# Half of the attention values computed inside the phase loop, and copied out by VectorE

## What is computed

```
q = (Q @ w_q.T).reshape(B, S, G, HG, HD)       # 8 groups of 4 heads, HD = 8
k = (K @ w_k.T).reshape(B, S, G, HD)
v = (V @ w_v.T).reshape(B, S, G, HD)
scores = jnp.einsum('bnghd,bmgd->bnghm', q, k) / scale
scores = jnp.where(causal, scores, NEG_INF)
attn = jax.nn.softmax(scores, axis=-1)
out = jnp.einsum('bnghm,bmgd->bnghd', attn, v).reshape(B, S, D)
return out @ w_o.T + b_o
```

## Time and profile before

| | |
|---|---|
| median of three runs | 400.14 us |
| the profiled execution's own time | 402.57 us |
| its span | 399.6 us |
| PE busy | 343.4 us (86%) |
| DVE busy | 210.5 us (53%) |
| ACT busy | 164.7 us (41%) |
| POOL busy | 100.9 us (25%) |

### The profile page before, as it was taken

How to read it: one execution, slowest core, us unless ns; L and a number is a source line. 1 busy time by engine, 2 the same in 40 slices (tenths; PEclk the granted TensorE clock), 3 DMA queues, 4 the chain that set the end, 5 groups by cost and what they waited for, 6 DMA issues and landing times.

```text
span 399.6 us, 4567 instructions
## 1 busy us (share of the span) xinstructions
PE 343.4 (86%) x1470; PEld 207.2 (52%) x1477; DVE 210.5 (53%) x501; ACT 164.7 (41%) x344; POOL 100.9 (25%) x156
## 2 busy tenths in 40 slices
PE   2999886529999847999799989988879989999997
PEld 1485675316665534555463655453343535444886
DVE  5143874502222267799436935792141339778921
ACT  2433443213333122246872875396785223333000
POOL 7102663520000377102340434045243001000000
PEclk9999997558999656999999999999999999999999
DMA  6995000152111127100000000000000000000011
GB/s 213 383 419 138 1 15 2 65 175 75 54 40 54 46 77 282 57 6 0 8 1 2 0 7 2 1 0 8 0 1 2 0 2 0 0 0 3 25 41 39
DMA packets 13880, 22.41 MB, mean 56 GB/s; under 512 B 2033, under 2 KB 11249, under 8 KB 13042
## 3 DMA queue, kind: packets, MB, share of 16 engines
q1 hardware_dynamic: 13090, 20.03, 14.5%
q0 software_dynamic: 768, 2.10, 1.6%
HBM read 15.83 MB, written 6.03 MB: 55 GB/s over the span
## 4 chain that ended last, share of the span: by engine, by line
PE 60%; DVE 16%; ACT 9%; issue 6%; POOL 4%; DMA 3%; another core or an unknown queue 0%; SPq 0%; ACTq 0%; DVEq 0%; POOLq 0%
PE bank L230 45%; DVE mx L1169 8%; ACT region L895 5%; PE bank L442 5%; PE bank L410 3%; POOL x_sorted L709 2%; PE bank L413 2%; DVE stats L966 2%; PE bank L243 1%; DVE x_sb L1006 1%; POOL rstd L682 1%; PE bank L237 1%; ACT qst L846 1%; DMA x_sb<-in_x_dram 1%; PE bank L490 1%
## 5 line engine op out<-in xcount | busy, mean ns | idle before, releaser
L1169 DVE TENSOR_REDUCE mx<-bank 128x2 f32<-128x512 f32 (+1 forms) x96 | 60.2, 684 | 13.9 <-PE bank L413 8.3
L895 ACT ACTIVATE region<-bank,padcol 128x512 f32<-128x512 f32 x96 | 60.7, 701 | 12.0 <-PE bank L230 11.0
L745 POOL TENSOR_SCALAR_AFFINE_SELECT region<-region 128x1024 f32<-128x1024 f32 x32 | 35.0, 1094 | 94.4 <-ACT region L895 94.0
L230 PE MATMUL bank<-xT,e_gu 128*128 128x512 f32 x128 | 57.6, 594 | 0.5 <-ACT xT L762 0.5
L230 PE MATMUL bank<-qst,kblk 128*128 128x512 f32 x96 | 46.0, 506 | 2.3 <-ACT amat L904 0.8
L410 PE MATMUL bank<-kblk,qst 128*128 128x512 f32 x96 | 44.3, 488 | 2.6 <-ACT qst L846 1.5
L230 PEld LDWEIGHTS bank<-xT,e_gu 128*128 128x128 f32 x128 | 23.4, 191 | 25.0 <-issue 24.2
L413 PE MATMUL bank<-causb,identb 128*128 128x256 bf16 (+1 forms) x89 | 28.9, 324 | 0.0
L678 POOL TENSOR_SCALAR veps<-mv 128x1 f32<-128x1 f32 x40 | 11.4, 286 | 67.3 <-DVE mv L968 65.1
L230 PE MATMUL bank<-e_down,region 128*128 128x256 f32 x128 | 27.8, 380 | 0.0
L1006 DVE SCALAR_TENSOR_TENSOR x_sb<-bank,tg,x_sb 128x256 f32<-128x256 f32 x24 | 11.6, 483 | 30.7 <-PE bank L230 30.6
(11 more groups left out here) (156 smaller groups left out, 551.9 us busy)
## 6 DMA issues: line engine op xcount, KB each, us to landing
e_gu<-in_e_gu_dram SPq DMA_DIRECT2D x2, 1408.0 KB, 12.6
x_sorted<-zero SPq DMA_DIRECT2D x1, 1920.0 KB, 10.2
y_sorted<-region SPq DMA_DIRECT2D x15, 128.0 KB, 1.7
x_sb<-in_x_dram SPq DMA_DIRECT2D x4, 256.0 KB, 4.0
ctxT<-in_ctxT_dram SPq DMA_DIRECT2D x2, 512.0 KB, 7.4
e_down<-in_e_down_dram SPq DMA_DIRECT2D x1, 1024.0 KB, 13.7
region<-x_sorted SPq DMA_DIRECT2D x1, 1024.0 KB, 7.4
e_gu<-in_f_gate_dram SPq DMA_DIRECT2D x1, 1024.0 KB, 4.9
```

The source lines that it names most:

```text
L230: return pe.matmul(dst, lhsT, rhs, start=first, stop=last)
L745: pool.affine_select(out=block, in_=block, compare_op=ALU.is_ge, fill=0.0, base=0, pattern=[[0, 2], [0, PER_GROUP], [1, P]], channel_multi ...
L895: taken(act.activation(dst, src.rearrange("p (h n) -> p h n", n=SEQ - mt * P), ACT.Exp, bias=padcol[:, key:key + 1], scale=float(HD) ** -0 ...
L1169: taken(dve.reduce_max(mx[:, b % 2, nt, quads, q, hg], src, AX), "sa")
```

## The change

`values` of the first half of the groups (q = 0) move from behind the loop to its steps 20 and 22, into a "max" bank each, and are read by a new DVE step `value_copy` instead of by ACT. Behind the loop stay the two `values` of the second half, with six `scores` behind each. The stage "av" is split in "av0" and "av1", with a semaphore pair each, and the waits on it follow.

```diff
+VALUES_AT = (20, 22)
+        VALUE_STAGES = ("av0", "av1")
-            def values(b, i):
+            def values(b, i, kind):
                 q, nt = divmod(i, 2)
+                stage = VALUE_STAGES[q]
                 if nt == 0:
                     pe.wait_ge(sem("causal_done"), 8 * b + 4 * q + 4)
-                dst = acquire(pe, "av", 4 * b + i, "wide")
+                dst = acquire(pe, stage, 2 * b + nt, kind)
...
                     if c == 0:
-                        pe.wait_ge(sem("av_taken"), 4 * b + 2 + nt + 1)
+                        for stage in VALUE_STAGES:
+                            pe.wait_ge(sem(stage + "_taken"), i + 1)
...
+                    if n in VALUES_AT:
+                        values(b, VALUES_AT.index(n), "max")
...
-                for i in range(4):
-                    values(b, i)
-                    for n in range(i * LEAD // 4, (i + 1) * LEAD // 4):
+                for i in range(2):
+                    values(b, 2 + i, "wide")
+                    for n in range(i * LEAD // 2, (i + 1) * LEAD // 2):
                         if b + 2 < BATCH:
                             scores(b + 2, n)
...
                 if n % 12 == 0 and b >= 1:
-                    act.wait_ge(sem("av_ready"), 4 * b - 2 + n // 6)
+                    act.wait_ge(sem(VALUE_STAGES[q] + "_ready"), 2 * b)
...
             def value_turn(b):
-                for q in range(HALVES):
-                    for nt in range(2):
-                        src = filled(act, "av", 4 * b + 2 * q + nt)
-                        if b >= 1:
-                            act.wait_ge(sem("avT_ready"), 8 * (b - 1) + 4 * nt + 4)
-                        taken(act.activation(avT[nt][:, q, :], src, ACT.Copy), "av")
+                for nt in range(2):
+                    src = filled(act, "av1", 2 * b + nt)
+                    if b >= 1:
+                        act.wait_ge(sem("avT_ready"), 8 * (b - 1) + 4 * nt + 4)
+                    taken(act.activation(avT[nt][:, 1, :], src, ACT.Copy), "av1")
...
+            def value_copy(b, nt):
+                src = filled(dve, "av0", 2 * b + nt)
+                if b >= 1:
+                    dve.wait_ge(sem("avT_ready"), 8 * (b - 1) + 4 * nt + 4)
+                taken(dve.tensor_copy(avT[nt][:, 0, :], src), "av0")
...
+                    if n in VALUES_AT:
+                        value_copy(b, VALUES_AT.index(n))
```

More of the change, by code:

```diff
@@ L443, in values @@
                                         start=(mt == 0), stop=(mt == nt), skip_group_check=True)
-                ready(ins, "av")
+                ready(ins, stage)
             def finish(b, n):
```

## The result

The change makes the kernel slower: 402.75 us in the median of 13 runs against 400.90 for the kernel before in 13 runs beside them, a ratio of 1.0064 with a 95% interval of [1.0048, 1.0081]. On another occasion it was 1.0063 [1.0041, 1.0084]. Forecast were +1.0 us (401.1) and a range of 398.5 to 403.6. 0.64% of 400.9 is 2.6 us, a little past the 2.0 us up to which I called it "the same"; the measured median lies outside the forecast's own range of 399.3 to 402.1 and at the 402.8 of rival C.

What follows compares the result with a forecast made beforehand. TensorE, busy 86% of the span, was taken as the bound, though not in the steps before the value blocks; phases of +1.3, 0.0, -0.1 and -0.2 summed to +1.0 us on the median 400.14: 401.1 us, range 398.5 to 403.6.

Steps and rivals of the forecast that it cites:

- rival C: Low clock on steps 20 to 23 of phase 2 or 3 costs 1.7 us: 402.8, 404.5 with two; chance 0.17.
- the second block: x16 at step 22, 1.85 us: more than three banks absorb, so phase 2's exponential 23 ends 1.28 us late.
- the last select: POOL's select behind exponential 23, 1.09 us, covered before, leaves PE idle 1.1 us in phases 2 and 3.
- the scores waited for ScalarE's value copies: Behind the stack in phases 0 and 1, rotation makes scores wait for ACT's copies; way still 1.2 and 1.3 us shorter.
- DVE's copy: Two value copies a phase move from ACT to DVE, taken as 0.69 us each, and cost nothing there.
- +1.3, 0.0, -0.1 and -0.2 us: Forecast changes of phases 0, 1, 2 and 3, summing to +1.0 us; phase 0's has the blocks at low clock.
- the forecast without the dip: Phase 0's low-clock stretch absent in both kernels: delay 1.45 not 2.5, net +0.2, sum -0.1, median 400.0 us.
- A weights matmul costs PE about 0.23 us: Price per weights matmul in the loop's steps, leaving PE some 0.35 us of air in each step.
- the first block: x8 at step 20, 1.00 us: in phase 2 hidden but for 0.16 us at exponential 21.
- B: Blocks hidden in steps 20 to 23, tails shorten by the full work: -5.3 us, 394.8; chance 0.13.
- D: Phases 0 and 1 gain nothing behind the stack, their delays of 2.5 and 1.3 stay: 403.6; chance 0.10.
- the bound of 2.0 in the forecast: Phase 1, way from stack to next loop: 2.0 us gained without the two waits for ACT's copies.

Runs made afterwards that it cites:

- e5: Changed kernel plus six unread bf16 matmuls on PE in phase 2, behind the weights of step 15, where PE waits for DVE; ratio 1.0019 to the kernel before.
- e6: Changed kernel with the value blocks of steps 20 and 22 copied by ScalarE, not DVE; one execution, no ratio, stages 0.6 us longer in all.
- e2: Changed kernel with only the x8 block in the loop, at step 20, x16 behind it copied by ScalarE, old bank rotation; 0.9979 of the kernel before.
- e4: The changed kernel unaltered, run again for comparison and a second trace; ratio 1.0063 to the kernel before.
- e1: Changed kernel with the bank rotation put back as before the change, by skipping one max and two wide turns per phase; 1.0003 of the kernel before.
- e7: Changed kernel, old rotation; in phases 2 and 3 x8 pieces at steps 20 and 22 and a third behind the loop; 0.9972 of the kernel before.
- before, second: The kernel before, unaltered, traced a second time; no ratio given, stages 34.92, 38.78, 26.79 and 22.51 us.
- e3: Changed kernel with the first half's values as three x8 pieces at steps 14, 18 and 22, old rotation; 0.9965 of the kernel before.
- before, third: The kernel before, unaltered, traced a third time; no ratio given, stages 35.51, 38.78, 25.81 and 22.49 us.
- e8: Changed kernel, old rotation; in phases 2 and 3 x8 pieces at steps 14 and 20 and a third behind the loop; 0.9948 of the kernel before.

## Why the prediction held, and where it was off

**Right.** That the change doesn't pay, and what each part does: the second block came through ScalarE's three banks to exponential 23, the last select came uncovered (PE waited 1.1 us for it in e5), the scores waited for ScalarE's value copies, and DVE's copy cost nothing. The value blocks stand as x8, x16 and x24.

**Luck in the number.** By stage the forecast was +1.3, 0.0, -0.1 and -0.2 us; the two first traces show +0.33, +0.23, +1.68 and -0.14. So +1.0 was in part made of a +1.3 that had the moved blocks inside a low stretch of phase 0, and no trace of the changed kernel has a stretch there; what phase 2 lost wasn't in it. Without low stretches the kernel before needs 34.92 + 38.78 + 25.81 + 22.50 = 122.0 us for the four stages and the changed one 35.86 + 39.04 + 26.14 + 22.36 = 123.4. The schedule alone costs 1.4 us, where the forecast without the dip had -0.1, too low by 1.5 and of the other sign.

**The term that was too small.** "A weights matmul costs PE about 0.23 us" holds behind another weights matmul or a transpose. Right behind a value block it takes 0.43 in the chain (273.56 and 276.30 in e5's chain; in the chain of the kernel before, the score at 211.22 behind a block has 0.43 too). That comes twice in a loop, at weights 21 and 23, and was left out of all four phases, which makes 1.6 us and so about the whole of the 1.5. The keys of phase 1 were late by 1.7 us, not 1.32, and phase 2 came to +0.32, not -0.1. Exponential 21 came 0.42 us later and not 0.16, so the first block was hidden less well than forecast, and exponential 23 came 1.7 us later against exponential 20, not 1.2 to 1.3, in phase 2 (e5) and in phase 3. The x24 block took 2.83 us in the chain, not 2.67. Phase 3 gained 0.14 where I had 0.2, but only because the 0.36 us gained at the DVE residual (e6) offset the same loss. No run shows why a matmul right behind a value block takes 0.2 us more. The row of the kernel before, behind the x16 block that ends at 211.22:

```profile
211.22 0.43 PE bank L410
```

**Phase 0.** I forecast +1.3 with the moved blocks inside a low stretch, and +0.2 without. The first of the two stands untested with two blocks; e2 had one block in a stretch, and its keys came 1.2 us later. The changed kernel's traces show no stretch there; keys come 2.0 us later than in the before trace that has none either (19.89 against 17.87) where I had 1.45; 0.4 of the difference is the term above. The way is 1.08 shorter, forecast 1.2. Net +0.94.

**The clock.** Rival C had the right mechanism: a stretch at 1.2 GHz on steps 20 to 23 of phase 2, where everything hangs on exponential 23; I priced it at 1.7 us and it cost 1.36. That 402.75 meets C's 402.8 is luck again, since C stood on a forecast with the stretch of phase 0 and with the term that was too small. All four traces with the changed kernel's schedule in phase 2 and no filler (after, e4, e6, and e1 at a slightly earlier place) have the stretch. But it isn't shown that the change brings more low clock: the mean granted clock over the runs was 0.934 in the 13 first ones and 0.931 for e4, and 0.932 for the kernel before beside e4. Before, a stretch fell in phase 0 in two of three traces and cost 0.6 us; after, it falls under blocks that the chain goes through. 1.4 of schedule and some 0.7 of clock (1.36 against 0.6 to 1.0) come to 2.1 us in the stages, and 124.74 less 122.64 from the two first traces is the same 2.1; the ratio says 2.6 with an interval of 1.9 to 3.2. Of this the 1.4 rests on traces that agree in their stages, and the 0.7 on where the stretch fell in single traces. e5, with the stretch taken away, has 0.8 us more than the first trace of the kernel before in its stages, and 0.8 by its ratio.

**The other rivals.** B fell: exponential 23 doesn't keep its pace. D fell: the way behind the stack is 1.0 and 1.5 us shorter, and 2.1 with the rotation put right, as the bound of 2.0 in the forecast had it.

**What goes with the low stretch of phase 2.** Not PE's wait alone, as e1 and e7 show, but also when the phase begins. Ahead of the attention phases the granted clock rises for the last time at about 160 us. Rows of the kernel before, then of the kernel after:

```profile
160.00:160.66 0.66, 0.66 (x4) 0.36 (x2) 0.00 (x0) 0.62 (x1) 0.00 (x0) 0.50 1.09 447
160.66:163.00 2.34, 2.32 (x11) 1.08 (x9) 2.29 (x4) 0.07 (x1) 0.00 (x0) 1.00 0.22 84
```

```profile
158.00:158.49 0.49, 0.49 (x3) 0.30 (x2) 0.00 (x0) 0.49 (x1) 0.00 (x0) 0.50 0.79 334
158.49:160.00 1.51, 1.44 (x7) 0.64 (x6) 1.34 (x3) 0.20 (x1) 0.00 (x0) 1.00 0.49 190
```

The time from this rise to phase 2's first exponential sorts the 12 traces:

| low stretch in phase 2 | us from the rise to phase 2's first exponential |
|---|---|
| yes | 96.34 (e1), 96.66 (before, second) |
| no | 97.13 (e7), 97.20 (e3), 97.24 (before, third), 97.25 (before, e2, e8) |
| yes | 97.92 (e6), 97.94 (after), 97.96 (e4) |
| no, with the filler | 97.98 (e5) |

The change lengthens phases 0 and 1 and so moves this time by 0.7 us, out of the group without a stretch. e4's loop began 2.6 us later than the first trace's, but so did the rise (161.05 and 158.49 us), hence the equal distance. The Trainium skill ("TensorE: Matmul & The Clock Gate", Part 1: The HAM clock gate) says that the window in which the chip watches TensorE runs freely against the kernel; the sorting fits that, and doesn't prove it. It was found in traces made for other ends: no run moved the beginning of phase 2 alone, and e5 alone shows the filler at work. In phase 0 the same time doesn't sort the traces: the three with a stretch have 22.92 to 22.96 us, and e4, e6 and the second of the kernel before have 22.96 and none.

## What to carry to other kernels

Work moved into "idle" slots of a loop is hidden only as far as the queue between the producer and the bound engine is deep: here three banks at 0.58 us each hid a block of 1.0 us but for 0.4, and not one of 1.85. Look too at what the moved work used to cover (here POOL's last select), and leave one piece there. When buffers rotate, count the turns again after every move: two banks handed out in another order cost 1.7 us by the stages, and with them put back the ratio fell from 1.006 to 1.000. Price a matmul by its neighbour, too: one term of 0.2 us, twice in each of four phases, was about the whole error of the schedule.

## What the runs showed of the hardware

A stretch at the 1.2 GHz level costs what its place makes of it, 0.6 us in phase 0 and 1.36 in phase 2 for the same 3.4 us. With six bf16 matmuls that nobody reads, 1.5 us on PE in a wait, the trace had no such stretch in phase 2 and the ratio was 1.0019, against 1.0063 without them. A 128x512 weights matmul right behind a block of value matmuls took 0.43 us in the chain, and 0.23 behind another weights matmul.
